# Second expert stage fed from attention's token order: its normalisation and logits beside and behind attention, half of its low weight halves kept in DRAM

## The chip, the cores and the metric

The kernel runs on one core of a Trainium2 chip. The metric is the device time of one execution in microseconds (us): before the change the median of three runs is 1264.93 us (1262.17 to 1265.98). The engines of the core run side by side, each through its own list of instructions, and wait for each other by semaphores: TensorE (PE) for matrix products and transposes, VectorE (DVE), ScalarE (ACT), GpSimd (POOL), and SyncE (SP), which here only starts transfers. POOL starts the indirect ones.

## The reference, cut to what matters

Six blocks, each on a layer norm of x (4 x 512 tokens of 256 numbers), each added to x. The change touches the attention (second) and the experts (first and third, with the same weights).

```python
x = x + 0.5 * ffn(layernorm(x), gate_w, gate_b, w1, b1, w2, b2)    # experts, stage 0
x = x + attn(layernorm(x), Wqkv, bqkv, Wout, bout)                 # causal attention, 16 heads
x = x + 0.5 * ffn(layernorm(x), gate_w, gate_b, w1, b1, w2, b2)    # experts, stage 1
x = x + 0.5 * hadamard_ffn(layernorm(x), W1, W2, W3)
x = x + feature_attn(layernorm(x), ...)
x = x + 0.5 * hadamard_ffn(layernorm(x), W1, W2, W3)

def ffn(x, gate_w, gate_b, w1, b1, w2, b2):
    logits = x @ gate_w.T + gate_b                 # 8 experts
    top_vals, top_idx = top_k(logits, 2)
    routing = softmax(top_vals)
    for e in range(8):
        h = x @ w1[e].T + b1[e]                    # 256 -> 512
        y = h[:, 0::2] * sigmoid(1.702 * h[:, 0::2]) * (h[:, 1::2] + 1.0)
        out += (y @ w2[e].T + b2[e]) * weight_of(routing, top_idx, e)
```

## The kernel before, in words

All matrix products that matter are exact to about fp32: each operand is split into a high half (rounded, made by ACT) and a low half (the rest, made by DVE), and three of the four products are summed.

x stays in the core's memory (SBUF) as 16 tiles of 128 tokens, four tiles to a "batch" (b = 0 to 3). In stage 0 and in attention tile t holds tokens t*128 to t*128+127 ("token order", `by_tiles`). Stage 1 and what follows want partition p to hold 16 neighbouring tokens (`by_sixteens`). So at its end attention writes x to DRAM (`x_turned`, L988), waits, reads it back in the other order (L992), waits again, and only then does the stage close. Every stage ends in a barrier of all engines in which its semaphores are cleared.

An expert stage (`experts_stage`, `which` = 0 or 1) runs like this. SP loads the small constants and eight records of weights (768 KB each, `record`, L410) and stores the normalised rows xn (L415). For each batch DVE makes the statistics (L91, L96), POOL the reciprocal root (L102, L105), DVE normalises (L114), PE transposes (L125), ACT and DVE split (L131, L136), PE computes the gate products (L484 to L489), ACT copies them out (L625), PE adds and transposes them to logits (L498), and DVE picks the best two (`choose`, L712 to L722). When all four batches are chosen, a routing chain on DVE and PE (L749 to L836) sorts 4096 token copies into 40 slots of 128 rows, one expert each. POOL then gathers the rows of xn by index (L456), two slots to a pair, and PE runs through 20 pairs (`turn`, `first`, `turn_y`, `second`), after which POOL scatters the results to DRAM (L462). Before the first pair PE waits for all eight low weight halves (`lo_split`, DVE L706: two in `choose`'s neighbourhood, two during the token sums, four after the indices), for the bias rows, and for the owners of the slots. At the end SP reads the results back (L431) and DVE adds them to x with the routing weights (L910).

Attention goes through 96 steps, three to each pair of heads, 24 (`WIDTH`) to each batch; `ALL` is 96. In step t, PE makes the scores (L1139), DVE their maxima (L1487); seven steps later (`LAG`) PE makes the transposed scores (L1154), ACT the exponentials (L1366), POOL masks them (L1041), and later still PE weighs the values (L1169). The steps also carry the projections of the next batch and the tail (sums, context, output projection, addition to x) of the last. Steps 96 to 107 are the drain, in which only the late parts of batch 3 run; behind the loop follow batch 3's sums (L1179), context (L1186), output projection (L1196) and addition (L1514). The order on each engine is the order in which the code is written, step by step; no scheduler moves anything.

Of the kernel before, what the change touches and what calls it, by code (L numbers as in the profile page):

```python
# [14 lines left out]
P = 128  # L15
# [29 lines left out]
def f32(ap):  # L45
    return ap.bitcast(F32)
# [22 lines left out]
class Norm:  # L69
# [28 lines left out]

    def rstd(self, pool, b):
# [39 lines left out]

def program(nc, ins, out):  # L140
# [4 lines left out]
    with ExitStack() as ctx:  # L145
# [23 lines left out]
        g.minus_low = sb("minus_low", [P, 1])  # L169
        g.xn_dram = nc.dram_tensor("xn_rows", (TOKENS, D), F32, kind="Internal").ap()  # L170
# [100 lines left out]
def experts_stage(nc, g, ins, which, x_dram):  # L271


    with ExitStack() as ctx:
# [5 lines left out]
        gate_w = sb("gate_w", [P, KC, E])  # L280
        gate_r = sb("gate_r", [P, KC, 2, E], F32R)
        both = sb("both", [2 * E, E])
        across = sb("across", [2 * E, 2, SEQ])
        b1_all = sb("b1_all", [P, E, 2 * IC])
        gate_b = sb("gate_b", [P, E])
        iota = sb("iota", [P, E])
        logits = sb("logits", [P, TILES, E])
        top = sb("top", [P, TILES, 8])
        top_at = sb("top_at", [P, TILES, 8], U32)
# [57 lines left out]
        rec_here = [sem(f"rec_here{e}") for e in range(E)]  # L347
        b1_here, b1_filled = sem("b1_here"), sem("b1_filled")
        pool_const, hi_split, lo_split, zeroed = sem("pool_const"), sem("hi_split"), sem("lo_split"), sem("zeroed")
        gate_split, logits_ready, logits_added = sem("gate_split"), sem("logits_ready"), sem("logits_added")  # L350
        gates_ps, gates_out, both_done = sem("gates_ps"), sem("gates_out"), sem("both_done")
        top_done, at_done = sem("top_done"), sem("at_done")
# [14 lines left out]
        norm = Norm(nc, sem, g, "norm", BATCH)  # L367
# [23 lines left out]
        def _(sp):  # L391
            if which == 0:
# [5 lines left out]
            sp.dma_start(gate_w[:, :, :], ins["gate_w"]).then_inc(small_here, 16)  # L398
            sp.dma_start(gate_b[:, :], ins["gate_b"].rearrange("(a e) -> a e", a=1).partition_broadcast(P)) \
                .then_inc(small_here, 16)  # L400
            sp.dma_start(iota[:, :], ins["iota"]).then_inc(small_here, 16)
            sp.wait_ge(zeroed, 1)
            for r in (0, LO_ROW):
                sp.dma_start(b2_src[r:r + E, :], ins["b2"]).then_inc(b2_here, 16)

            sp.dma_start(b1_all[:, :, :], ins["moe"].rearrange("e p n -> p e n")[:, :, REC_W1 + REC_W2:REC]) \
                .then_inc(b1_here, 16)

            def record(e):
                sp.dma_start(f32(w[1][:, e, :]), ins["moe"][e][:, 0:REC_W1 + REC_W2]).then_inc(rec_here[e], 16)  # L410
            for e in range(E // 2):
                record(e)
            for b in range(BATCH):
                sp.wait_ge(norm.xn_done, b + 1)
                sp.dma_start(by_tiles(g.xn_dram[:, :], b), g.xn[:, b, :, :]).then_inc(xn_stored, 16)  # L415
                record(E // 2 + b)
            sp.wait_ge(owner_done, 1)
            for j, (hi, _, source) in enumerate(jobs):
                if j:
                    sp.wait_ge(later_hi, j)  # L420
                    sp.wait_ge(later_lo, j)
                sp.dma_start(later[:, 0:hi.shape[1]], source).then_inc(later_here, 16)
            if which == 1:
                sp.dma_start(w3_raw[:, :, :], ins["w3"]).then_inc(w3_here, 16)
            for s in range(2):
                sp.wait_ge(scattered[s], 16 * PAIRS)
            for b in range(BATCH):
                if b >= 2:
                    sp.wait_ge(combined, 2 * (b - 1) + 1)
                for r in range(2):  # L430
                    sp.dma_start(back[:, b % 2, r, :, :], by_tiles(g.made_dram[r * TOKENS:(r + 1) * TOKENS, :], b)) \  # L431
# [1869 lines left out]
```

## Time and profile before

| | us |
|---|---|
| median of three runs | 1264.93 |
| the profiled execution, its own time | 1265.17 |
| its span, first to last instruction | 1263.4 |
| PE busy over the span | 1038.3 (82%) |
| DVE, ACT, POOL busy | 737.3, 461.0, 448.0 |

The stages follow each other without overlap. In the profiled execution stage 0 runs until about 227 us, attention until about 549 us, stage 1 until about 773 us, and the rest is the Hadamard and feature stages. A row of the timeline gives start, busy time, engine, line, operation, output and inputs, how many instructions were merged into it (x8), and in brackets how long the engine had been idle before it and which instruction ended that wait. A SPq row is SP starting a transfer, not the transfer. PEclk is the granted clock of PE, 1.0 being 2.4 GHz and 0.5 being 1.2 GHz.

### The profile page before, as it was taken

How to read it: one execution, taken by the hardware profiler on the slowest of the kernel's cores; microseconds unless marked ns; L12 is line 12 of the kernel's file. 1: busy time of each engine (PE TensorE's matmuls, PEld its weight loads, DVE VectorE, ACT ScalarE, POOL GpSimd, SP SyncE). 2: the span in 40 equal slices, each digit the busy share in tenths (PEclk: the TensorE clock that was granted, in tenths of full speed). 3: DMA queues.
4: the chain of work that ended last, by engine and by line, in shares of the span. 5: the costliest groups of instructions: out<-in, count | busy, mean ns of one | idle time of the engine just before them, and what ended most of it. 6: DMA issues, size and time to landing. Idle time of an engine off the chain costs nothing. (4 is left out here: it accounts for less than half of the span.)

```text
span 1263.4 us, 18069 instructions
## 1 busy us (share of the span) xinstructions
PE 1038.3 (82%) x6196; PEld 844.0 (67%) x6196; DVE 737.3 (58%) x1753; ACT 461.0 (36%) x804; POOL 448.0 (35%) x482
## 2 busy tenths in 40 slices
PE   4469992459999999624599993999989999789997
PEld 3358882346566666313488882888878888678886
DVE  5854443457777777157454436565646667655554
ACT  3314331127666766224143321322323333222231
POOL 2046652435353622120366630000127879500000
PEclk9579997667999999765699996999986999989999
DMA  9013224000000000082142233000010030000001
GB/s 333 3 59 110 88 80 160 22 1 1 2 1 18 1 18 5 30 244 91 46 173 86 89 113 105 1 1 1 1 67 1 1 67 1 1 1 17 18 6 29
DMA packets 38524, 66.03 MB, mean 52 GB/s; under 512 B 8195, under 2 KB 29732, under 8 KB 38054
## 3 DMA queue, kind: packets, MB, share of 16 engines
q1 hardware_dynamic: 30758, 43.90, 10.9%
q0 software_dynamic: 7680, 20.98, 5.1%
q8 instruction: 54, 0.88, 0.3%
q14 instruction: 32, 0.26, 0.1%
HBM read 43.89 MB, written 20.97 MB: 51 GB/s over the span
## 5 line engine op out<-in xcount | busy, mean ns | idle before, releaser
L1698 PE MATMUL ps<-xt,w 128*128 128x512 f32 x768 | 194.4, 404 | 5.6 <-PEq L66 3.2
L1698 PEld LDWEIGHTS ps<-xt,w 128*128 128x128 f32 x768 | 143.9, 193 | 36.5 <-DVE xt L136 6.2
L1487 DVE CUSTOM_DVE_ANT_0 ps<-ps,att_mask 128x128 f32<-128x128 f32 (+3 forms) x256 | 119.1, 516 | 39.7 <-PE ps L1139 39.5
L559 PE MATMUL ps<-moe_w,moe_narrow_xb 128*128 x480 | 126.8, 400 | 0.0
L456 POOL DMA_INDIRECT moe_xs<-xn_rows,moe_index x80 | 81.0, 1012 | 129.2 <-DVE moe_index L836 85.7
L1794 DVE TENSOR_TENSOR had_gated<-ps,had_sig 128x512 f32<-128x512 f32 x64 | 44.2, 691 | 120.1 <-ACT had_sig L1751 120.1
L102 POOL TENSOR_TENSOR var_eps<-bn,eps 128x4 f32<-128x4 f32 x24 | 5.2, 218 | 297.3 <-DVE bn L96 297.3
L462 POOL DMA_INDIRECT made_rows<-moe_units_made,moe_index x80 | 81.2, 1015 | 77.4 <-ACT moe_units_made L669 65.2
L1751 ACT ACTIVATE had_sig<-ps 128x512 f32<-128x512 f32 x64 | 38.4, 600 | 187.0 <-PE ps L1698 187.0
L559 PEld LDWEIGHTS ps<-moe_w,moe_narrow_xb 128*128 128x128 f32 x480 | 92.7, 194 | 19.2
L853 DVE TENSOR_TENSOR moe_narrow_xb<-ps,moe_narrow_xb 128x512 fp32r<-128x512 f32 x40 | 27.7, 692 | 128.9 <-ACT moe_narrow_xb L651 128.9
L1366 ACT ACTIVATE att_early_probs<-ps 128x384 f32<-128x384 f32 (+1 forms) x192 | 90.9, 527 | 29.0 <-PE ps L1154 27.7
L1710 PE MATMUL ps<-w,had_yhi 128*128 128x256 f32 x512 | 93.3, 280 | 1.8 <-DVE had_ylo L1806 1.8
L1041 POOL TENSOR_SCALAR_AFFINE_SELECT att_early_probs<-att_early_probs 128x256 f32<-128x256 f32 x128 | 53.3, 429 | 114.2 <-ACT att_early_probs L1366 113.9
L651 ACT ACTIVATE moe_narrow_xb<-ps 128x512 fp32r<-128x512 f32 x40 | 23.9, 598 | 177.9 <-PE ps L543 177.9
L1710 PEld LDWEIGHTS ps<-w,had_yhi 128*128 128x128 f32 x512 | 82.4, 188 | 8.0 <-DVE had_ylo L1806 2.6
L1139 PE MATMUL ps<-att_kt,att_q 48*128 48x128 f32 (+3 forms) x256 | 65.5, 413 | 9.4 <-DVE att_q_stack L1487 6.8
L2004 PE MATMUL ps<-fea_wv_prod,ident 128*128 128x256 f32 x256 | 68.3, 429 | 5.0 <-DVE fea_wv_prod L2194 5.0
L1710 PE MATMUL ps<-w,had_ylo 128*128 128x256 f32 x256 | 71.7, 280 | 0.0
L1924 POOL TENSOR_TENSOR fea_inv_norm<-fea_norm,neg_half 128x24 f32<-128x24 f32 x16 | 66.7, 4172 | 5.7 <-DVE fea_norm L2152 5.7
L585 PE MATMUL ps<-moe_w,moe_units_yb 128*128 x480 | 68.7, 283 | 0.0
L2004 PEld LDWEIGHTS ps<-fea_wv_prod,ident 128*128 128x128 f32 x256 | 54.2, 216 | 15.0 <-DVE fea_wv_prod L2194 6.2
(249 smaller groups left out, 2266.9 us busy)
## 6 DMA issues: line engine op xcount, KB each, us to landing
moe_w<-in_moe SPq DMA_DIRECT2D x16, 768.0 KB, 8.6
moe_w<-made_rows SPq DMA_DIRECT2D x16, 512.0 KB, 4.9
xn_rows<-moe_wide_xn SPq DMA_DIRECT2D x8, 512.0 KB, 9.5
x<-x_turned SPq DMA_DIRECT2D x8, 512.0 KB, 7.8
x<-in_x SPq DMA_DIRECT2D x4, 512.0 KB, 5.4
x_turned<-x SPq DMA_DIRECT2D x4, 512.0 KB, 2.9
moe_narrow_later<-in_w SPq DMA_DIRECT2D x4, 512.0 KB, 3.4
x_turned<-x SPq DMA_DIRECT2D x1, 2048.0 KB, 8.2
```

The costliest lines, as they stand in the source:

```text
L456: nc.gpsimd.indirect_dma_start(out=xs[:, j % 2, i, :], out_offset=None, in_=g.xn_dram[:, :], in_offset=at(0, 2 * j + i)).then_inc(gathered ...
L462: nc.gpsimd.indirect_dma_start(out=g.made_dram[:, :], out_offset=at(1, 2 * j + i), in_=made[:, j % 2, i, :], in_offset=None) \
L559: last = nc.tensor.matmul(h_bank(j, i), xb[a][:, j % 2, i, k, :], weight(c), start=False, stop=(k == KC - 1 and c == 1))
L585: last = nc.tensor.matmul(O_BANK[:, i * D:(i + 1) * D], yb[a][:, j % 2, i, c, :], weight(q), start=False, stop=(c == IC - 1 and q == 1), s ...
L1041: last = nc.gpsimd.affine_select(block, block, [[0, 2], [1, P]], ALU.is_ge, 0.0, base=0, channel_multiplier=-1)
L1139: last = nc.tensor.matmul(g.ps[:, a, col:col + n], q1[at, w % 2, i * P:n], kt[at, w % 4, 0:n], start=True, stop=True)
L1366: nc.scalar.activation(probs[:, w % 3, a, at:at + n], g.ps[:, 2 + a, 0:n], ACT.Exp, scale=HD ** -0.5).then_inc(exp_done, 1)
L1487: last = nc.vector.tensor_tensor_reduce(g.ps[:, a, col:col + n], g.ps[:, a, col:col + n], mask[:, SEQ - n:SEQ], -1.0, 3.0e38, ALU.add, ALU ...
L1698: last = nc.tensor.matmul(g.ps[:, bank(n, half), :], w[a][:, k, c * P:(c + 1) * P], xt[low][:, b % 2, k, :], start=(k == 0 and q == 0), st ...
L1710: last = nc.tensor.matmul(o, a[:, n % 4, at], g.w2[w][:, c, :], start=(c == 0 and q == 0 and i % 2 == 0), stop=(c == HC - 1 and q == 2), s ...
L1924: nc.gpsimd.tensor_tensor(inv_norm[:, t % 4, :], norm2[:, t % 4, :], g.neg_half[:, 0:QKH], ALU.pow) \
L2004: last = nc.tensor.matmul(g.ps[:, 5 + t % 2, 0:D], g.ident[:, :], wv_prod[:, t % 2, k, :, :].rearrange("p h d -> p (h d)"), start=(k == 0) ...
```

## The change

- **Token order.** Routing of stage 1 is made in attention's token order. Attention no longer reads x back at its end; SP reads it in the other order in the middle of stage 1's expert loop, after the second of the later weights. The results are read back `by_sixteens`. The routing weights, made in token order, are turned by a small way round: PE transposes them (32 x 128), ACT copies them out, SP stores them to DRAM and loads them back in the other order (`route_rows`, `route_back`).
- **Normalisation for stage 1 moves into attention**, as a second `Norm` named `after` and a class `Choice` with the four steps from gate products to the best two. For batches 0 and 1 DVE makes it in pieces, one after the maxima of each step of the last batch (u = 1 to 8 and 9 to 16): four of one tile's statistics, one for the variances, one empty, two of two tiles' normalisation. Batch 2 follows in steps 97 and 100. Transposes, splits, gate products, logits and choice of batches 0 to 2 stand in the drain (`AFTER`: they begin at steps 97, 99 and 102, the gate products two steps later, the logits three). Batch 3 has all of it behind attention's last addition. The normalised rows take the place of attention's own and of `rot`.
- **Low halves.** Stage 0, once its eight low halves are made, writes those of experts 4 to 7 to DRAM (`low_weights`). Stage 1 reads them back instead of making them, and makes only four on DVE.
- **Order within stage 1.** SP starts with the records. ACT makes the routing weights and then the eight high halves and the biases. PE turns the biases after the token sums. DVE makes the bias rows after the owners.

The diff, cut:

```diff
@@ Norm @@
+    def stats_of_tile(self, b, i, x_block):
+        self.nc.vector.bn_stats(self.g.bn6[:, self.slot(b), i, :], x_block(i)).then_inc(self.stats_done, 1)
+    def variance(self, dve, b, stats_done):       # bn_aggr x4
+    def normalise_tiles(self, b, tiles, x_block): # tensor_scalar for each tile
+class Choice:    # gates, out_of_gates, logits_of, choose: the code of experts_stage, moved
@@ experts_stage, SP @@
+            def stored_low(e):
+                sp.dma_start(f32(w[1][:, e, :]), g.low_dram[e - E // 2]).then_inc(low_here[e], 16)
+            else:
+                record(0)
+                record(1)
+                biases()
+                for e in range(2, E):
+                    record(e)
+                for e in range(E - LOADED, E):
+                    stored_low(e)
+                sp.wait_ge(rows_out, 1)
+                sp.dma_start(g.route_dram, route_rows[:, :]).then_inc(rows_stored, 16)
+                sp.wait_ge(rows_stored, 16)
+                sp.dma_start(route_back[:, :, :], ...).then_inc(route_here, 16)
             sp.wait_ge(owner_done, 1)
+            if which == 0:
+                sp.wait_ge(lo_split, E)
+                for e in range(E // 2, E):
+                    sp.dma_start(g.low_dram[e - E // 2], f32(w[1][:, e, :])).then_inc(low_stored, 16)
...
+                if which == 1 and j == 1:
+                    for b in range(BATCH):
+                        sp.dma_start(g.x[:, mine, :], by_sixteens(g.turned_dram[0])[:, mine, :]).then_inc(x_here[b], 16)
@@ experts_stage, PE @@
-            pe.wait_ge(lo_split, E)
+            if which == 1:
+                turn_biases()
+                pe.wait_ge(route_done, 2)
+                nc.tensor.transpose(g.ps[0:2 * TILES, 7, 0:P], route[...], g.ident[:, :]).then_inc(route_turned, 1)
+            pe.wait_ge(hi_split, E)
+            pe.wait_ge(lo_split, E - LOADED)
+            if which == 1:
+                for e in range(E - LOADED, E):
+                    pe.wait_ge(low_here[e], 16)
@@ attention_stage @@
+        AFTER = ((5, ALL + 1), (0, ALL + 3), (5, ALL + 6), (2, None))
-            for b in range(BATCH):
-                at = slice(b * BATCH_P, (b + 1) * BATCH_P)
-                sp.dma_start(g.x[at, :, :], by_sixteens(g.turned_dram[0])[at]).then_inc(x_turned, 16)
-            sp.wait_ge(x_turned, 16 * BATCH)
+            for b in range(BATCH):
+                sp.wait_ge(xn_stored[b], 16)
@@ PE, in the loop @@
+                for m in at_step(t, 3):
+                    choice.logits_of(pe, m, bank_of(m) + 1)
+                for m in at_step(t, 2):
+                    choice.gates(pe, m, bank_of(m))
+                for m in at_step(t, 0):
+                    turn_after(m)
+            pe.wait_ge(choice.gates_out, 2)
+            pe.wait_ge(choice.logits_added, 2)
@@ DVE, in the loop @@
+                for m in range(2):
+                    if 0 <= u - 1 - 8 * m < 8 and b == BATCH - 1:
+                        after_piece(m, u - 1 - 8 * m)
@@ DVE, behind the loop @@
+            after_whole(BATCH - 1)
+            after.low(dve, BATCH - 1, bank_of(BATCH - 1), xt[0][:, :, :], xt[1][:, :, :])
+            choice.choose(dve, BATCH - 1, bank_of(BATCH - 1) + 1)
```

On PE, the end of the drain and what is behind it stood like this before (`att_summed` are batch 3's weighted values, `wout` the output projection):

```order
L1154 MATMUL ps<-att_q,att_kt 128x128
L1169 MATMUL ps<-att_early_probs,att_v 17x128 x4
L1169 MATMUL ps<-att_early_probs,att_v 17x256 x4
L1169 MATMUL ps<-att_early_probs,att_v 17x384 x4
L1169 MATMUL ps<-att_early_probs,att_v 17x512 x4
L1179 MATMUL ps<-ident,att_summed 128x128 x16
L1186 MATMUL ps<-ident,att_context 128x128 x8
L1196 MATMUL ps<-wout,att_ct 128x256 x24
```

The same place now (`att_turns_after_xn` are rows normalised for stage 1, `gate_r` the split gate weights, `both` the small matrix that adds the two halves of the gate products):

```order
L197 MATMUL ps<-both,att_qk 128x8 x4
L142 MATMUL ps<-ident,att_turns_after_xn 128x128 x8
L1318 MATMUL ps<-att_early_probs,att_v 17x128 x4
L1318 MATMUL ps<-att_early_probs,att_v 17x256 x4
L178 MATMUL ps<-att_xt,gate_r 16x512
L180 MATMUL ps<-att_xt,gate_r 8x512 x2
L182 MATMUL ps<-att_xt,gate_r 16x512
L1318 MATMUL ps<-att_early_probs,att_v 17x384 x4
L1318 MATMUL ps<-att_early_probs,att_v 17x512 x4
L197 MATMUL ps<-both,att_qk 128x8 x4
L1328 MATMUL ps<-ident,att_summed 128x128 x16
L1335 MATMUL ps<-ident,att_context 128x128 x8
```

Batch 2's transposes, gate products and logits now stand between and around the last weighings; those of batches 0 and 1 stand the same way further up.

On DVE, between the slot rows and the first pair of the expert loop of stage 1, before:

```order
L816 TENSOR_TENSOR moe_wide_slot_row<-column,moe_pos 128x2048 x2
L706 TENSOR_TENSOR moe_w<-moe_w 128x1536 x2
L823 TENSOR_SCALAR moe_narrow_index_f<-ps 128x40
...
L846 TENSOR_SCALAR moe_owner_row<-moe_owner,row_e 128x40
L706 TENSOR_TENSOR moe_w<-moe_w 128x1536 x4
```

And now:

```order
L931 TENSOR_TENSOR moe_wide_slot_row<-column,moe_pos 128x2048 x2
L826 TENSOR_TENSOR moe_w<-moe_w 128x1536 x3
L938 TENSOR_SCALAR moe_narrow_index_f<-ps 128x40
...
L961 TENSOR_SCALAR moe_owner_row<-moe_owner,row_e 128x40
L859 SCALAR_TENSOR_TENSOR moe_b_row<-moe_units_b_hi,minus_low,ps 128x512
L861 SCALAR_TENSOR_TENSOR moe_b_row<-moe_units_b_hi,minus_low,moe_units_b_src 128x256
L826 TENSOR_TENSOR moe_w<-moe_w 128x1536
```

Three low halves stand ahead of the indices, and one, with the bias rows ahead of it, behind the owners, where there were four.

On SP, stage 1 from its start to the first of the later weights, now:

```order
L491 DMA moe_w<-in_moe 128x1536 x2
L499 DMA moe_units_b_src<-in_b 8x256 x2
L500 DMA moe_b_all<-in_moe 128x8x4
L491 DMA moe_w<-in_moe 128x1536 x6
L494 DMA moe_w<-low_weights 128x1536 x4
L523 DMA route_rows<-moe_route_rows 32x128
L525 DMA moe_route_back<-route_rows 128x2x16
L536 DMA moe_narrow_later<-in_had 128x256
```

Before, the small constants stood first, then four records, and each of the other four stood behind the store of one batch of normalised rows.

## Rows read from the trace of the kernel before

**Rows 1.** Timeline, seam from attention to stage 1: start, us, engine, what, [idle before].
```profile
532.36 0.69 DVE L1514 TENSOR_TENSOR x<-x,ps 128x512 f32<-128x512 f32 x1 [1.14 <-PE ps L1196]
...
549.38 1.40 DVE L91 BATCH_NORM_STATS2 bn<-x 128x6 f32<-128x256 f32 x4 [16.34 <-PEq L66]
```

**Rows 2.** Timeline of stage 1, POOL and PE, at the start of the expert loop.
```profile
604.91 1.09 POOL L456 DMA_INDIRECT moe_xs<-xn_rows,moe_index  x1 [41.97 <-DVE moe_index L836]
606.30 1.79 POOL L456 DMA_INDIRECT moe_xs<-xn_rows,moe_index  x1 [0.30 <-issue]
612.33 1.11 PE L543 MATMUL ps<-ident,moe_xs 128*128 128x128 f32 x4 [9.49 <-DVE moe_w L706]
```

**Rows 3.** Timeline of stage 1, DVE, from batch 3's logits to the low halves.
```profile
583.39 0.18 DVE L712 TENSOR_TENSOR moe_logits<-ps,moe_gate_b 128x32 f32<-128x32 f32 x1
584.57 0.17 DVE L749 TENSOR_TENSOR moe_margin<-moe_top 128x16 f32<-128x16 f32 x1
602.88 0.20 DVE L823 TENSOR_SCALAR moe_narrow_index_f<-ps 128x40 f32<-128x40 f32 x1 [1.57 <-PE ps L528]
605.52 6.76 DVE L706 TENSOR_TENSOR moe_w<-moe_w 128x1536 fp32r<-128x1536 f32 x4
```

**Rows 4.** Stretches: start:end, length; busy (count) of five engines, PEclk, DMA share, GB/s.
```profile
453.00:503.00 50.00, 48.55 (x395) 30.31 (x393) 39.35 (x147) 33.59 (x69) 12.63 (x32) 1.00 0.04 12
503.00:521.50 18.50, 14.07 (x91) 5.54 (x89) 0.69 (x1) 8.30 (x17) 3.92 (x10) 0.72 0.09 29
613.00:749.00 136.00, 126.61 (x756) 109.51 (x755) 58.84 (x87) 49.75 (x86) 76.58 (x76) 0.97 0.29 98
```

**Rows 5.** Stage 1, groups by shape, 549 to 586 us: xcount | busy us, mean ns.
```profile
L91 DVE BATCH_NORM_STATS2 bn<-x 128x6 f32<-128x256 f32 x16 | 5.6, 410 | 16.3 <-PEq L66 16.3
L114 DVE TENSOR_SCALAR moe_wide_xn<-x,bn,rstd 128x256 f32<-128x256 f32 x16 | 5.4, 402 | 0.0
L96 DVE BATCH_NORM_AGGREGATE bn<-bn 128x2 f32<-128x6 f32 x16 | 1.6, 159 | 0.6 <-issue 0.2
```

**Rows 6.** Timeline of stage 1: transposes, low split, gate products, copy and logits of single batches.
```profile
555.01 1.97 PE L125 MATMUL ps<-ident,moe_wide_xn 128*128 128x128 f32 x8 [22.75 <-DVE moe_gate_r L740]
558.07 1.22 DVE L136 TENSOR_TENSOR moe_narrow_xt<-ps,moe_narrow_xt 128x1024 fp32r<-128x1024 f32 x1
559.69 0.78 PE L484 MATMUL ps<-moe_narrow_xt,moe_gate_r 128*16 128x512 f32 x1
561.78 0.59 ACT L625 ACTIVATE moe_across<-ps 16x512 f32<-16x512 f32 x1 [0.68 <-PE ps L489]
562.41 1.10 PE L125 MATMUL ps<-ident,moe_wide_xn 128*128 128x128 f32 x8 [0.67 <-DVE moe_wide_xn L114]
564.58 1.05 PE L498 MATMUL ps<-moe_both,moe_across 16*128 16x8 f32 x8
579.81 1.87 PE L498 MATMUL ps<-moe_both,moe_across 16*128 16x8 f32 x8
```

**Rows 7.** Timeline, PE: weighings L1169, 16 in the loop and 32 after it.
```profile
496.59 1.70 PE L1169 MATMUL ps<-att_early_probs,att_v 128*17 128x384 f32 x16
516.39 4.47 PE L1169 MATMUL ps<-att_early_probs,att_v 128*17 128x128 f32 x32 [1.41 <-POOL att_early_probs L1041]
```

**Rows 8.** Timeline of DVE over the barrier between stage 1 and the next stage.
```profile
773.41 1.40 DVE L91 BATCH_NORM_STATS2 bn<-x 128x6 f32<-128x256 f32 x4 [1.23 <-PEq L66]
```

**Rows 9.** Stretches as in Rows 4, while weights and rows move.
```profile
555.00:575.00 20.00, 13.39 (x60) 8.78 (x60) 13.90 (x58) 9.86 (x10) 3.03 (x6) 0.74 1.03 390
561.00:563.00 2.00, 1.33 (x7) 0.59 (x6) 2.00 (x7) 1.32 (x3) 1.70 (x4) 0.76 0.88 259
573.00:575.00 2.00, 0.00 (x0) 0.00 (x0) 1.93 (x14) 0.52 (x1) 0.00 (x0) 1.00 1.10 431
```

**Rows 10.** Gathers L456, all 80 of them.
```profile
DMA to landing us min/median/max: 2.6/2.8/5.5
```

**Rows 11.** Timeline of DVE at the end of stage 1: the additions wait for the results.
```profile
756.48 6.67 DVE L910 SCALAR_TENSOR_TENSOR x<-moe_w,moe_route,x 128x256 f32<-128x256 f32 x16 [6.99 <-DMA moe_w<-made_rows]
```

More of the change, by code:

```diff
@@ L440, in _ @@
             pool.wait_ge(zeroed, 1)
-            for b in range(BATCH):
-                norm.rstd(pool, b)
+            if which == 0:
+                for b in range(BATCH):
+                    norm.rstd(pool, b)
             pool.wait_ge(b1_here, 16)
@@ L493, in logits_of @@
-            def logits_of(b):
-                pe.wait_ge(gates_out, b + 1)
-                if b >= 2:
-                    pe.wait_ge(logits_added, b - 1)
-                for i in range(BT):
-                    last = nc.tensor.matmul(g.ps[:, b % 2, i * E:(i + 1) * E], across[:, b % 2, i * P:(i + 1) * P],
-                                            both[:, :], start=True, stop=True)
-                last.then_inc(logits_ready, 1)
-            norm.turn(pe, 0, 4)
-            norm.turn(pe, 1, 6)
@@ L818, in _ @@
                     .then_inc(spread, 1)
-            for e in range(2, 4):
+            for e in range(2 - 2 * which, 4 - which):
                 low_weights(e)
@@ L847, in _ @@
                 .then_inc(owner_done, 1)
-            for e in range(4, E):
+            if which == 1:
+                bias_rows()
+            for e in range(4 - which, E - LOADED):
                 low_weights(e)
@@ L1379, in high_context, with high_after @@
                 nc.scalar.activation(ct[0][:, k, :], g.ps[:, bank, :], ACT.Copy).then_inc(chi_done, 1)
+            def high_after(m):
+                if m == 0:
+                    act.wait_ge(v_ps, 4 * BATCH)
+                else:
+                    act.wait_ge(choice.gates_ps, m)
+                after.high(act, m, bank_of(m), xt[0][:, :, :])
             act.wait_ge(consts, CONSTS)
@@ L1583, in _ @@
                     maxima(t)
+                for m in range(2):
+                    if 0 <= u - 1 - 8 * m < 8 and b == BATCH - 1:
+                        after_piece(m, u - 1 - 8 * m)
+                for m in at_step(t, 3):
+                    choice.choose(dve, m, bank_of(m) + 1)
+                for m in at_step(t, 0):
+                    after.low(dve, m, bank_of(m), xt[0][:, :, :], xt[1][:, :, :])
+                if t == ALL + 1:
+                    for piece in range(BT + 1):
+                        after_piece(2, piece)
+                elif t == ALL + 4:
+                    for piece in range(BT + 1, BT + 4):
+                        after_piece(2, piece)
             for i in range(BT):
```

449 lines of the change are left out of this document (303 added, 146 removed).

## The prediction

> **What bounds the kernel now.** I read the busy tenths by slice first, then the busy time by stretches, then the timeline of all engines over the seam between attention and stage 1. Attention's steps and both expert loops are bound by PE: in the steps of the last batch PE is busy 48.55 of 50 us, and in stage 1's loop 126.61 of 136 [rows 4]. At the seam nothing of the sort holds. DVE's last addition of attention ends at 533.05 us. Then x goes to DRAM and comes back (L988, L992), and DVE starts stage 1 at 549.38, having stood still for 16.3 us [rows 1]. The normalisation and the choice of four batches last until DVE's L749 at 584.57; the routing chain leads to the index at 602.88 and the first gather at 604.91; and the first transposes of the expert loop start at 612.33, held by the last four low halves (605.52 + 6.76 = 612.28) [rows 2, 3]. So from 533.05 to 612.33, 79.3 us, the kernel hangs on a chain of waits and PE mostly stands still. The change is about this chain, and its worth is the move of the time 612.33.
>
> **The chain after the change**, link by link, on the clock of the trace of before.
>
> First, *attention until 533.05*. In the last batch's steps DVE gets the pieces of two batches: statistics, variances and normalisation cost 5.6 + 1.6 + 5.4 = 12.6 us for four batches [rows 5], so 6.3 us for two. DVE is busy 39.35 us of those 50 [rows 4] and has 10.65 us free, but PE, with 1.45 us free, waits for DVE's maxima of the step before, so a piece in a step where DVE is late shows. I take 1 us; the ends are 0 (all in the gaps) and 6.3 (all exposed). POOL's part hides, since POOL is busy 12.63 of the 50.
>
> *The drain* (503 to 521.5) gets PE's, ACT's and DVE's work of three batches. Transposes, gate products and logits of one batch run without a gap from 562.41 to 564.58 + 1.05 = 565.63, which is 3.22 us at the upper clock; at the lower one they are 1.97 + (561.78 - 559.69 = 2.09) + 1.87 = 5.93 us [rows 6]. Three batches are 9.7 or 17.8 us. What can hide them: PE stands idle for 18.5 - 14.07 = 4.4 us of the drain, and its granted clock falls there to 0.72 [rows 4]. The 32 weighings of the last group take 4.47 us, while 16 of them at the upper clock took 1.70 [rows 7], so about 1.3 us, and as much again for the first group, come back if denser work keeps the clock up. The low end is 9.7 - 4.4 - 2.6 = 2.7 us, the high end 17.8. I take 5: near the low end, as PE gets work where it stood idle, yet above it, since ACT and PE hand the exponentials to and fro and new instructions stand between them in both orders; the last gate products and logits stand among the last weighings, with nothing to hide in. DVE, at 0.69 us busy, has room for all of its part. With the 1 us of the steps, the last addition ends at 533.05 + 6 = 539.1.
>
> *Batch 3* then has its whole chain alone. In stage 1 the same way took from 549.38 (statistics) over the transposes at 555.01 to the end of the low split at 558.07 + 1.22 = 559.29, 9.9 us; gate products to the end of the copy 561.78 + 0.59 - 559.69 = 2.7; logits 1.87; choice 584.57 - 583.39 = 1.2 [rows 1, 3, 6]. With three handovers of 0.05 it is 15.8 us, at the lower clock: PE will have been without work for some 6 us when the transposes come, as before those of 555.01, which ran at it. Were all of PE's part at the upper clock, 5.93 - 3.22 = 2.7 us would go. Attention ends at 539.1 + 15.8 = 554.9. Storing the last rows is started about 5 us after the addition and lies beside the other 10. The barrier costs 1.23 us [rows 8], so DVE starts stage 1 at 556.1 instead of 549.38. What was gained by leaving out the turn of x (16.3 us) is thus about paid away by batch 3's chain and the drain: minus 6.7.
>
> *Routing* starts at once. From L749 to the first gather took 604.91 - 584.57 = 20.3 us [rows 2, 3]. A third low half ahead of the index costs 0.1: DVE waited 1.57 us there, and a half takes 6.76 / 4 = 1.69 [rows 3]. The bias rows that stood ahead of the scan lay beside PE's ranks, so they give nothing. The first gather goes out 20.5 us after the stage's start, its partner 1.4 later, and it lands after 2.8 [rows 2, 10]: the rows of the first pair are there after 24.7 us. The biases are made on ACT behind the eighth high half (about 21 us, as records arrive), DVE's bias rows and last low half then end at about 25. These two ends fall together.
>
> *The weights* are the third. Stage 1 now moves twelve blocks of 128 x 1536 x 4 B = 0.786 MB, 9.44 MB in all, where it moved eight and four stores. While such transfers kept the DMA engines full, from 555 to 575, they moved 390 GB/s; two stretches of it moved 259 and 431 [rows 9]. At 390 GB/s it is 24.2 us. Ahead of it I put 2 us from start to first bytes and 1 for the tiny bias pieces, behind it 1 for landing: 28.2 us. At 431 it would be 25.9, at 259 it would be 40.4. The four low halves come last in SP's queue and PE waits for all of them, so my value is that they end the wait: the first transposes at 556.1 + 28.2 = 584.3. That is 28.0 us before 612.33.
>
> The trace gives 390 GB/s [rows 9]. The Trainium skill (DMA: Bandwidth & Descriptors, Bandwidth) holds that HBM limits such reads to about 358 GB/s for one core; this trace is above that, so the row decides, and by the page's figure the load would take 26.4 us and the sum be 2.2 us higher. By another section of that page (Issuing engines are not separate DMA queues), POOL's gathers run on the same 16 engines as SP's transfers and interleave with them; no row of before shows the two together here, and by it the first gathers would land later without being last.
>
> **The rest.** Stage 0 writes 3.1 MB: some 8 us of transfers at the start of its loop. Stage 1's loop gets 2 MB of x and the small way round of the routing weights. In stage 1's loop the DMA share is 0.29 with PE busy 93% of the time [rows 4], so there is room: 0, up to 3 if gathers come late. Behind the loop DVE waited 6.99 us for the results [rows 11]; they now come in pieces of 4 KB instead of 1 KB. I take 0.5 us less, between 1.5 less and 1 more. The ceiling is that DVE and ACT still have to turn the other weights.
>
> **The sum**, against the profiled execution's own 1265.17 (0.24 above the median of 1264.93): 1265.17 - 28.0 - 0.5 = 1236.7, so 1237 us.
>
> **Rivals.**
> *A: the weights are not last.* For it: full stretches at 431 GB/s bring the load to 25.9 us, and gathers and DVE end near 25. Against: the mean over 20 us is 390. The loop would start at about 25.5 instead of 28.2: 1237 - 2.7 = 1234. With PE at the upper clock in batch 3's chain too it would be 1231.5.
> *B: attention pays more.* The drain is paid at the lower clock (13.7 after what little hides) and the steps at half their pieces (3). For it: the clock of 0.72 in the drain, and ACT, which is one list for exponentials and the new copies. Against: PE's idle 4.4 us. That is 16.7 instead of 6: 1237 + 10.7 = 1248.
> *C: slower than before, by the weights.* In before four of the eight low halves cost DVE 6.8 us at the end; now they are 3.1 MB more to read, behind everything. The point from which it decides is a first transposes later than 612.8, 56.7 us into the stage: 9.44 MB in 52.7 us, 179 GB/s. At 150 GB/s, 63 us, it would be 1265.17 + 10 - 0.5 = 1275. For it: rates fell to 259 once, and the low halves are read from a buffer that no row shows being read. Against: that stretch was 2 us long, and the reads have 6 KB a partition like the records.
> *D: the seam does not shorten*, because batches 0 to 2 wait in the drain for each other and everything lands behind the loop: from transposes to choice a batch takes 15.8 - 5.6 (549.38 to 555.01 [rows 1, 6]) = 10.2 us, three of them 30.6 in place of my 5: 1262.6, within what can be told. Against: the steps between them give each hop one or two steps of time.
>
> **How the numbers follow.** The forecast, weights last and 4 to 9 us paid in attention, has 0.55, from 1233 to 1241; A 0.17; B 0.22; C 0.03; D 0.03. The range has to leave out no more than 2 in 10: it goes from 1229 to 1249, taking in A whole and most of B. A measurement of this kernel can tell about 0.3%, 3.8 us, from no change. Slower by more than that is C, 0.03; within it D and the neighbourhood, 0.02; the rest, 0.95, is faster.
>
> **What would show it.** In the profile after: the last addition of x at about 539, with PE's clock in the drain over 0.8; the first rows of stage 1's DVE at about 556, an idle time of about 1.2 before them; the first gather 20 to 21 us later, and PE's first transposes of gathered rows 28 us later, put down to a transfer of `moe_w`, not to DVE; the distance from there to the end of the kernel as before, less about half a us. It is wrong if the steps of the last batch grow by more than 3 us, if the drain grows by more than 9, if the wait ahead of the expert loop ends with the gather or with a low half made by DVE (A), or if the loop itself, 613 to 745 before, is no longer of the same length.

## The result and the profile after

The changed kernel takes 1253.33 us (median of 20 runs, 1246.21 to 1262.62), the one before 1265.43 (20 runs); the ratio is 0.9898, interval 0.9881 to 0.9915. It is faster, by 1.0% instead of the 2.2% forecast: 1253.3 lies above 1237 and above the range's end of 1249. The profiled execution took 1256.92 us with a span of 1254.7.

First the timeline of the seam (start, us, engine, what, idle before), which answers to [rows 1, 6, 8]:

```profile
555.70 0.69 DVE L1700 TENSOR_TENSOR x<-x,ps 128x512 f32<-128x512 f32 x1 [1.87 <-PE ps L1345]
561.12 1.94 PE L142 MATMUL ps<-ident,att_turns_after_xn 128*128 128x128 f32 x8 [5.53 <-issue]
565.50 0.61 PE L178 MATMUL ps<-att_xt,gate_r 128*16 128x512 f32 x1 [2.43 <-DVE att_xt L153]
568.06 1.87 PE L197 MATMUL ps<-both,att_qk 16*128 16x8 f32 x8 [0.68 <-ACT att_qk L189]
572.41 0.19 DVE L865 TENSOR_TENSOR moe_margin<-top 128x16 f32<-128x16 f32 x1 [1.17 <-PEq L66]
...
592.32 1.09 POOL L579 DMA_INDIRECT moe_xs<-xn_rows,moe_index  x1 [10.78 <-DVE moe_index L951]
600.31 1.08 PE L653 MATMUL ps<-ident,moe_xs 128*128 128x128 f32 x4 [8.39 <-DMA moe_w<-low_weights]
```

The last addition of attention ends at 556.39, where 539.1 was forecast. From there the chain runs as forecast: 16.0 us to stage 1's first work on DVE at 572.41 (17.0 forecast), 19.9 to the first gather (20.5), 27.9 to the first transposes of gathered rows (28.2), and these wait for the transfer of the low halves, as forecast. Before, the way from the last addition to these transposes was 79.3 us; now it is 43.9. The seam works. What was lost was lost ahead of it, in attention.

The stretches of attention (start:end, length; busy and count of PE, weight loads, DVE, ACT, POOL; PE's granted clock, DMA share, GB/s) answer to [rows 4]. They run from one batch's last addition to the next: batch 2's steps, batch 3's steps, the drain; then stage 1's load and the stretch of the loop in which x is read:

```profile
395.00:459.70 64.70, 62.77 (x468) 42.32 (x468) 46.36 (x158) 42.56 (x88) 28.86 (x49) 0.95 0.03 9
459.70:518.00 58.30, 55.56 (x396) 33.95 (x396) 44.80 (x172) 33.95 (x70) 15.06 (x36) 0.85 0.08 28
518.00:555.70 37.70, 32.06 (x192) 20.22 (x192) 15.26 (x67) 13.50 (x25) 5.06 (x12) 0.73 0.09 28
...
576.40:598.40 22.00, 8.17 (x37) 7.69 (x37) 19.75 (x29) 12.81 (x11) 6.84 (x6) 0.50 1.01 398
...
623.00:640.00 17.00, 14.15 (x77) 12.17 (x76) 6.97 (x11) 6.25 (x10) 8.90 (x9) 0.90 0.68 248
```

The same three stretches of attention in the kernel before:

```profile
391.60:453.40 61.80, 59.81 (x468) 39.85 (x468) 46.32 (x159) 42.45 (x88) 28.89 (x49) 1.00 0.03 10
453.40:503.40 50.00, 48.55 (x394) 30.31 (x394) 39.38 (x148) 33.59 (x69) 12.63 (x32) 1.00 0.04 12
503.40:532.40 29.00, 21.32 (x136) 12.28 (x134) 5.12 (x13) 9.41 (x19) 3.92 (x10) 0.76 0.06 19
```

PE does the same matmuls in the steps of batch 3, yet is busy for 55.6 us instead of 48.6: its granted clock is 0.85 instead of 1.00 (of the two levels, 2.4 GHz all the time before, and 1.2 GHz for part of it now). DVE has 5.4 us more to do, where the prediction counted 6.3. PE's own standing still grew by only 1.3 us, and the view of waits of PE in this stretch (what waited for what: us in total, times, longest) names it. First after, then before:

```profile
PE ps L1258 <- DVE att_kt L1663: 1.3, 3, 0.7
PE ps L1288 <- DVE att_q_stack L1673: 0.7, 3, 0.3
```

```profile
PE ps L1139 <- DVE att_q_stack L1487: 0.7, 3, 0.3
```

New are three waits for DVE's copy of K into `kt` (L1663). PE waits for it because the copy reads the bank of the accumulator memory (PSUM) into which PE's next transposes (L1258) go. The copy opens every third step, so eight of them stand among the 24 steps. In six of them one of the new pieces stands right ahead of the copy, and in three of these six the copy comes late. The longest wait, with the normalisation of two tiles ahead of the copy:

```profile
497.98 0.82 DVE L112 TENSOR_SCALAR att_turns_after_xn<-x,bn,rstd 128x256 f32<-128x256 f32 x2
498.72 0.68 DVE L1663 CAST att_kt<-ps 128x512 fp32r<-128x512 f32 x1
499.54 0.63 PE L1258 MATMUL ps<-ident,att_q_stack 128*128 128x128 f32 x4 [0.69 <-DVE att_kt L1663]
```

The loop itself (first transposes to SP's last request for results) has grown from 137.1 to 140.2 us, and in it PE waits once for a gather, while x is read:

```profile
PE ps L653 <- DMA moe_xs<-xn_rows,moe_index: 2.4, 1, 2.4
```

At the loop's end DVE waits 5.97 us for results instead of 6.99 [rows 11].

### The profile page after: what moved, and what is told of

It reads as the page before. It is cut to its first block and busy times, and to the rows that moved or that the text cites. A ratio compares the mean times of both kernels' runs of the same rounds, so it can differ in the third digit from the quotient of the medians.

```text
span 1254.7 us, 18084 instructions
## 1 busy us (share of the span) xinstructions
PE 1052.2 (84%) x6197; PEld 855.9 (68%) x6197; DVE 728.8 (58%) x1745; ACT 462.3 (37%) x805; POOL 450.5 (36%) x482
## 5 line engine op out<-in xcount | busy, mean ns | idle before, releaser
L1927 PE MATMUL ps<-xt,w 128*128 128x512 f32 x768 | 191.6, 400 | 5.6 <-PEq L66 3.2
L1288 PE MATMUL ps<-att_kt,att_q 48*128 48x256 f32 (+3 forms) x256 | 66.8, 428 | 9.8 <-DVE att_q_stack L1673 7.2
```

Source lines behind the costliest of these rows:

```text
L1288: last = nc.tensor.matmul(g.ps[:, a, col:col + n], q1[at, w % 2, i * P:n], kt[at, w % 4, 0:n], start=True, stop=True)
L1927: last = nc.tensor.matmul(g.ps[:, bank(n, half), :], w[a][:, k, c * P:(c + 1) * P], xt[low][:, b % 2, k, :], start=(k == 0 and q == 0), st ...
```

## The experiments

Theory 1: DVE's pieces and the added work in the drain cost attention what is missing, the pieces mostly by way of PE's granted clock; and x's 2 MB cost the loop 3 us. Its rival: these executions had a poorer clock by chance, and the pieces lie in DVE's gaps. All times are medians; ratios are against the kernel before on the same chip. "Steps" are those of batch 3, "drain" is from batch 2's last addition to batch 3's.

**e1_no_pieces**
```
 def after_piece(m, piece):
+    if m < 2:
+        if piece == BT: nc.vector.bn_aggr(...)      # one, to release POOL
...
+if t in (ALL, ALL + 1):                             # start of the drain
+    after.normalise_tiles(t - ALL, range(BT), ...)
```


> Leaves out, of batches 0 and 1, the statistics and variances, and takes their normalisation (from old statistics) out of the steps of the last batch and puts it at the start of the drain, where DVE is idle. All else is as in the changed kernel. Theory 1 (the pieces on DVE show in the steps): the 24 steps of the last batch, from batch 1's last addition to batch 2's, took 50.0 us before and 57.9 after; here they come back by most of the 6.3 us that the pieces cost DVE, to about 52, and the whole takes about 1247 us. Theory 2 (the steps were slow because the granted clock was lower in this execution, by chance or because PE waited a little more, and the pieces lie in DVE's gaps): the steps stay above 56 us wherever the granted clock in them is below 0.9, and the whole stays at about 1253.

1248.38 us, ratio 0.9878 (0.9841 to 0.9915). The steps:

```profile
451.10:502.50 51.40, 49.99 (x394) 31.11 (x394) 39.55 (x149) 33.53 (x69) 15.06 (x36) 0.97 0.03 11
```

51.5 us with the clock at 0.97, and the waits for L1663 are gone, so theory 1 holds for the steps. The drain, into which the normalisation of two batches was moved, took 38.3 us in this execution.

**e2_no_drain**
```
-for m in at_step(t, 3): choice.logits_of(pe, m, bank_of(m) + 1)
-for m in at_step(t, 2): choice.gates(pe, m, bank_of(m))
-for m in at_step(t, 0): turn_after(m)
...                                                  # ACT's and DVE's parts too
```


> Leaves out, in the drain, the transposes, the split, the gate products, the logits and the choice of batches 0 to 2 (batch 3's are made as before and take batch 0's place); the pieces on DVE stay. Theory 1 (work that goes into the drain is paid for nearly in full, 8.7 us where 5 were forecast): from batch 2's last addition to batch 3's it is 29 us again instead of 37.7, and the whole takes about 1244.5 us. Theory 2 (the drain is longer because PE's granted clock fell in it to 0.77 and its chain of hand-overs between PE, ACT and DVE has the same length without the added work): it stays at 33 us or more and the whole takes 1249 or more.

1241.23 us, ratio 0.9789 (0.9754 to 0.9824), 12.1 below the changed kernel. The drain:

```profile
518.90:545.20 26.30, 18.83 (x132) 11.38 (x132) 8.34 (x24) 9.12 (x19) 5.08 (x12) 0.87 0.12 41
```

26.4 us: less than the 29.0 of before, at a better clock. So the added work costs 8.6 us against the 35.0 that the drain takes in five of the six executions whose attention is that of the changed kernel (below). Theory 1 holds: 26.4 us is even below the 29 that it expected. The steps here took 61.0 us at a clock of 0.80, with the three waits: these have nothing to do with the drain.

**e8_again** (the changed kernel once more)

> The changed kernel once more, word for word. If the steps of the last batch are slow by the change itself, they take 57 to 59 us again with PE's granted clock at 0.85 to 0.88; if that was the chance of one execution, they come out nearer to the 50.0 us of before. The way from the loop's first transposes to SP's last request for results is 140 us again if it is the change's, 137 if it was chance. The whole: 1253.

1252.42 us, ratio 0.99 (0.9855 to 0.9944).

```profile
389.30:454.00 64.70, 62.74 (x466) 42.31 (x467) 46.38 (x158) 42.54 (x88) 28.83 (x49) 0.95 0.03 9
454.00:515.00 61.00, 58.15 (x396) 35.05 (x396) 45.12 (x171) 34.00 (x70) 15.07 (x36) 0.80 0.08 27
515.00:550.00 35.00, 29.30 (x192) 19.88 (x192) 15.30 (x67) 13.55 (x25) 5.04 (x12) 0.81 0.09 31
```

The long steps are the change's, not one execution's. The drain's 37.7 us was partly chance: here it is 35.0, 6.0 more than before. The loop takes 140.6.

**e10_before_again** (the kernel before once more)

> The kernel before once more, word for word. Its profiled execution had attention's last 24 steps in 50.0 us and the loop of the second expert stage in 137.1. If the change made both longer, they come out at 50 to 51 and at 136.5 to 137.5 again; if chance of an execution did, at least one of them moves towards the changed kernel's 57 to 61 and 140 to 141. The whole: 1265.

1267.98 us, ratio 1.0011 (0.9979 to 1.0043).

```profile
455.40:505.40 50.00, 48.19 (x388) 29.84 (x386) 39.38 (x148) 33.80 (x70) 12.63 (x32) 1.00 0.04 12
505.40:534.50 29.10, 21.09 (x132) 12.39 (x132) 5.16 (x13) 9.08 (x19) 3.92 (x10) 0.77 0.06 19
613.81:752.25 138.44, 129.49 (x761) 113.06 (x762) 59.27 (x87) 49.75 (x86) 76.66 (x76) 0.95 0.29 96
```

50.0 and 29.0 us again, to 0.05. The loop is 138.4, so part of its 3 us may be chance of one execution: this point came out between the two outcomes.

**e5_fine**
```
-for m in range(2):
-    if 0 <= u - 1 - 8 * m < 8 and b == BATCH - 1: after_piece(m, u - 1 - 8 * m)
+for m, piece in {2 * WIDTH + 3: ((0, 0),), 2 * WIDTH + 4: ((0, 1),), ...
+                 3 * WIDTH + 3: ((0, 5),), 3 * WIDTH + 5: ((0, 6),), ...
+                 ALL: ((1, 5), (1, 6), (1, 7), (1, 8))}.get(t, ()):
+    fine_piece(m, piece)                            # one tile each
```


> Nothing is left out; DVE's pieces of batches 0 and 1 are placed anew. Batch 0's statistics and variances go into the steps of batch 2, its normalisation goes tile by tile into the steps of batch 3, never into a step right ahead of one that opens with the copy of K (L1663), batch 1's statistics likewise, and batch 1's normalisation goes to the start of the drain. In the changed kernel PE waited three times for that copy (1.3 us) and its granted clock was 0.85 in these steps. Theory 1 (the pieces cost through those waits: PE stands still for a moment and its granted clock falls behind each, so that PE's busy time grows from 48.6 to 55.6 us): without the waits the steps from batch 1's last addition to batch 2's come back to 50 to 52 us, as where the pieces were left out, and the whole takes about 1247 us. Theory 2 (any 6 us more on DVE, wherever they lie, slow PE by lateness of the maxima): the steps stay above 55 us and the whole at 1251 or more.

1246.12 us, ratio 0.9848 (0.9807 to 0.9889).

```profile
391.80:456.30 64.50, 62.46 (x468) 42.13 (x467) 48.33 (x167) 42.68 (x88) 30.33 (x51) 0.95 0.03 10
456.30:506.70 50.40, 48.95 (x394) 30.22 (x394) 41.71 (x160) 33.60 (x69) 14.03 (x34) 1.00 0.07 22
```

The cut leaves out the matching move of POOL's reciprocal roots. DVE still does 2.3 us of new work in the steps (and 2 us in those of batch 2), but the steps take 50.4 us at the full clock, and the waits for L1663 are gone: PE's waits in this stretch are those of before.

```profile
PE ps L1288 <- DVE att_q_stack L1673: 0.7, 3, 0.3
```

Over all profiled executions: in six without the waits for L1663 the steps took 50.0 to 52.0 us (50.0, 50.0, 50.4, 51.5, 51.8, 52.0); in eight with them 57.5 to 61.0, at clocks from 0.80 to 0.88. Theory 1 holds. One rival is not excluded: this run also leaves less than half of DVE's 5.4 us in these steps (the rest went to batch 2's steps and the drain), so placement and amount were changed together, and no run has all of it in these steps clear of the copies.

The traces tell in which order waits and clock came. In the profiled run of the changed kernel the waits for L1663 ended at 472.23, 486.24 and 499.54, and PE's clock fell in three stretches:

```profile
463.90:467.30 3.40, 3.40 (x29) 2.13 (x28) 1.52 (x6) 1.20 (x3) 0.45 (x2) 0.50 0.01 2
474.10:480.90 6.80, 6.80 (x39) 3.84 (x40) 5.12 (x19) 3.48 (x8) 2.47 (x5) 0.50 0.01 2
501.40:508.20 6.80, 6.80 (x38) 4.85 (x42) 4.31 (x17) 4.54 (x10) 1.58 (x4) 0.50 0.00 0
```

The second and the third stretch begin 1.9 us behind a wait. So it is in all eight executions with the waits: each stretch of 6.8 us at 0.50 in these steps begins 1.5 to 3.0 us behind one of them, and 18 of the 24 waits have one. The first stretch above stands ahead of the first wait. Four of the eight have such a short one there, and e1_no_pieces, e11_fine_tail and e12_fine_three_tail have one each without any wait for L1663, with steps of 51.5 to 52.0 us. So 1.5 to 2 us of the profiled run's 8.3 need not come from these waits (an estimate from those lengths).

What theory 1 does not explain are batch 2's steps. PE has the same waits there in either kernel (the longest 0.7 to 0.8 us), and except in the three runs with finer pieces their code is unchanged. Yet they took 61.8 us in both executions of the kernel before and 63.4 to 64.9 in all twelve others, with the mean clock at 0.95 to 0.97 instead of 1.00. The 2.9 us that they cost in the profiled run stay open.

**e7_tail**
```
 turn_context(BATCH - 1, 1, 6)
+turn_after(2)
 project_half(BATCH - 1, 0, 0)
 project_half(BATCH - 1, 1, 1)
+choice.gates(pe, 2, bank_of(2))
+choice.logits_of(pe, 2, bank_of(2) + 1)
```


> Batch 2's transposes, gate products, logits and choice are moved out of the drain's last weighings to behind the context of batch 3, where its output projection and the statistics of batch 3 are under way; nothing is left out. Theory 1 (PE's work that was added to the drain is paid nearly in full at the low clock, and batch 3's chain behind it has gaps of 5.5 and 2.4 us in which PE waits): from batch 2's last addition to the choice of batch 3, 52.6 us in the changed kernel, 2 to 3 us are saved and the whole takes about 1250.5. Theory 2 (the chain of hand-overs is the bound, not PE): the same length within 1 us, 1253.

1244.29 us, ratio 0.9841 (0.98 to 0.9882). The timeline of PE at the end of attention shows batch 2's transposes (first line) between context and projection, and its logits ahead of batch 3's transposes:

```profile
543.28 1.04 PE L142 MATMUL ps<-ident,att_turns_after_xn 128*128 128x128 f32 x8
545.02 3.14 PE L1345 MATMUL ps<-wout,att_ct 128*128 128x256 f32 x24 [0.70 <-DVE att_ct L1695]
548.00 0.40 PE L178 MATMUL ps<-att_xt,gate_r 128*16 128x512 f32 x1
549.76 1.05 PE L197 MATMUL ps<-both,att_qk 16*128 16x8 f32 x8 [0.68 <-ACT att_qk L189]
553.69 1.94 PE L142 MATMUL ps<-ident,att_turns_after_xn 128*128 128x128 f32 x8 [2.88 <-issue]
```

What stood in the way of the drain now fills a gap of batch 3's chain: PE stands still for 2.88 us ahead of that batch's transposes instead of 5.53, and the work there runs at the upper clock (1.04 us for eight transposes, 1.94 at the lower one). From batch 2's last addition to batch 3's choice it is 45.7 us, 4.0 less than in e8_again: theory 1, by more than its 2 to 3 us. The median fell by 8.1; the rest I can't place, since in the profile it lies in later, unchanged stages (506.6 us after SP's request, 512.9 in e8_again, 506.4 in e10_before_again), which vary that much by themselves.

**e3_all_low**
```
-LOADED = E // 2 if which == 1 else 0
+LOADED = 0                                          # and no store in stage 0
```


> No low half goes to DRAM: all eight are made by DVE in stage 1 as before the change, four of them after the bias rows; stage 0 stores none and stage 1 reads none back. Theory 1 (weights last, as the prediction had it): the load is then 6.3 MB instead of 9.4 and no longer last; DVE ends last: the low half that ended at 594.92 + 1.75 = 596.7 is followed by 6.8 us of four more, so the first transposes of gathered rows come 31 us after the stage's start instead of 27.9, 3.1 us more, put down to DVE. Against it stand the 1.7 us that stage 0 grew by, if its stores caused them: the whole takes 1253.3 + 3.1 - 1.7 = 1254.7 us. Theory 2 (the stores cost stage 0 nothing and what it grew by is chance): 1256.4 us, stage 0 as long as in the changed kernel.

1254.56 us, ratio 0.9909 (0.9878 to 0.9939), the same within the error.

```profile
597.37 1.08 PE L651 MATMUL ps<-ident,moe_xs 128*128 128x128 f32 x4 [11.54 <-DVE moe_w L824]
```

That is 31.05 us after the stage's start at 566.32, held by DVE: theory 1's 31. Keeping low halves in DRAM is thus worth 3 us. Its store costs nothing that can be seen: from stage 0's first transposes of gathered rows to attention's start it is 157.6 us here and 156.7 to 158.2 in the eleven executions that store four halves or three. The 1.7 us that attention started late were chance; that part of theory 1 fell.

**e6_three**
```
-LOADED = E // 2 if which == 1 else 0
+LOADED = 3 if which == 1 else 0                     # and three stores in stage 0
```


> Three instead of four of the low halves go to DRAM and back; DVE makes the fifth in stage 1, behind the bias rows. Theory 1 (the prediction's: the load is last by far, and DVE would end at 26.0 us after the stage's start, 24.3 and 1.75): the load is 0.79 MB shorter, 2.0 us at 390 GB/s, so the first transposes come 26.0 us after the stage's start instead of 27.9, and the whole takes about 1251.5. Theory 2 (the load's rate is set by something that another low half on DVE or the gathers disturb, or DVE ends later than the sum): they come at 27 or later, and put down to DVE.

1252.01 us, ratio 0.9899 (0.9858 to 0.9939).

```profile
591.07 1.09 PE L653 MATMUL ps<-ident,moe_xs 128*128 128x128 f32 x4 [6.77 <-DVE moe_w L826]
```

26.3 us after the stage's start (564.80), against the forecast 26.0: theory 1 in the length, though DVE is now last. The median shows none of it: the loop of this execution took 142.0.

**e4_x_spread**
```
-if which == 1 and j == 1: (four reads of x, one behind the other)
+for b in range(BATCH):
+    sp.wait_ge(x_turned, 11 + 2 * b)
+    (the read of batch b)
```


> The 2 MB of x that stage 1's loop reads back at its second pair are asked for one batch at a time, behind pairs 11, 13, 15 and 17. Theory 1 (the block of 2 MB holds up the gathers of three pairs, whose rows PE waited 5.8 us for between 625 and 640): the way from the first transposes of the loop to SP's last request for results goes from 140.2 us to the 137.1 of the kernel before, and the whole takes about 1250.5 us. Theory 2 (the waits are only moved, since DVE and ACT's turned weights and PE set the loop's pace on average): it stays at 139 to 141 us and the whole at 1253.

1250.95 us, ratio 0.989 (0.9861 to 0.9919). The loop took 139.8 us, theory 2: the wait for the gather shrank from 2.4 to 0.7 us, and others grew (for L985 from 0.5 to 2.2).

**e9_no_x**
```
-sp.dma_start(g.x[:, mine, :], ...)                  # 512 KB a batch
+sp.dma_start(g.x[:, mine, 0:128], ...)              # mine: one tile; 64 KB
```


> Leaves out nearly all of the read of x in the second expert stage's loop: of each batch 64 KB instead of 512 KB come back. Spread over the loop, the 2 MB had cost it the same as in one block (139.8 us from the first transposes to SP's last request for results, 140.2 to 140.6 in the changed kernel, 137.1 before). Theory 1 (it is the 2 MB themselves, wherever they lie, that delay gathers, and results by about 3 us): the way is 137 to 138 us. Theory 2 (the loop is longer by something else, such as the order in which the turned weights' requests stand behind the gathers or the chance of the granted clock): it stays at 139.5 or more.

1247.79 us, ratio 0.9863 (0.9822 to 0.9904).

```profile
590.77:726.84 136.07, 127.31 (x761) 110.21 (x762) 59.15 (x86) 49.76 (x86) 76.78 (x76) 0.97 0.31 101
```

The loop takes 136.1 us, theory 1, and 1 us under its range; the eleven executions that read x back took 139.5 to 142.0, the two of before 137.1 and 138.4. So it is the 2 MB themselves, wherever they lie. Their price is known only roughly, from one execution without them: 3.4 to 5.9 us against these eleven, and 3.8 against e4_x_spread, whose loop had nearly the same clock (0.98 against 0.97).

**e11_fine_tail** (the edits of e5_fine and e7_tail together)

> Two edits together, nothing left out: DVE's pieces of batches 0 and 1 placed clear of the copies of K, and batch 2's part moved behind the context of batch 3. Alone they gave medians of 1246.1 and 1244.3 us against the 1252.4 of the changed kernel. Theory 1 (they act in different stretches, the one on the steps' granted clock, the other on the drain, and add up): 1252.4 - 6.3 - 8.1 = 1238 us. Theory 2 (both win back the same granted clock, or part of the second's gain was chance in the later stages, whose 506.6 us were 6 less than in the changed kernel's second profile): about 1242.

1238.97 us, ratio 0.9777 (0.9736 to 0.9818): the two edits add up, which is theory 1, with steps of 52.0 us and a drain of 30.2 us.

**e12_fine_three_tail** (that and the edit of e6_three)

> As the kernel with DVE's pieces clear of the copies of K and batch 2's part behind the context of batch 3, and in addition three instead of four low halves by way of DRAM. Theory 1 (the first transposes come 1.7 us earlier after attention's end, as they did with this edit alone, and the rest keeps its length): 1.5 us less than the kernel without this edit. Theory 2 (the loop that starts earlier finds its gathers later, since with this edit alone the loop took 142.0 us instead of 140.6): no difference.

1236.49 us, ratio 0.9762 (0.9719 to 0.9804).

```profile
459.70:511.50 51.80, 50.05 (x388) 30.76 (x386) 41.84 (x160) 33.79 (x70) 14.03 (x34) 0.97 0.06 22
511.50:541.00 29.50, 26.08 (x182) 16.93 (x183) 15.34 (x57) 12.53 (x24) 5.12 (x12) 0.83 0.16 54
```
```profile
583.80 1.08 PE L653 MATMUL ps<-ident,moe_xs 128*128 128x128 f32 x4 [6.55 <-DVE moe_w L826]
```

Steps and drain are as in e11_fine_tail. From stage 1's start (557.75) to these transposes it is 26.05 us. Against e11_fine_tail the two intervals overlap, so the 2.5 us between them are not shown by the times alone, and neither theory is decided by them; the 26 us instead of 28 are, by this trace and e6_three's. This version beats both kernels: 2.4% under the one before, 1.3% under the changed one. That it lands at the forecast's 1237 says nothing for the forecast, which was made for the changed kernel's order of work.

## Why the prediction missed

| link, us (+ longer or later than before) | forecast | profiled run | e8_again |
|---|---|---|---|
| start of attention | 0 | +1.7 | -1.9 |
| from there to batch 0's last addition | 0 | +1.7 | -0.4 |
| batch 2's steps | 0 | +2.9 | +2.9 |
| batch 3's steps | +1 | +8.3 | +11.0 |
| drain | +5 | +8.7 | +6.0 |
| last addition to stage 1's start, length | 17.0 | 16.0 | 16.0 |
| stage 1's start to first transposes, length | 28.2 | 27.9 | 28.2 |
| loop | 0 | +3.1 | +3.5 |
| end of stage 1 | -0.5 | -1.2 | -1.0 |
| later stages | 0 | +1.4 | -0.1 |

*The step that failed* is the first: "so a piece in a step where DVE is late shows. I take 1 us; the ends are 0 (all in the gaps) and 6.3 (all exposed)". The delay itself was sized rightly: PE waited 1.3 us more. But the bound of 6.3 held only for delays at an unchanged clock. The eight executions with the three new waits show 7.5 to 11.0 us, above that end, since PE's granted clock fell, mostly right behind these waits, and its 48.6 us of work became 54.1 to 58.2. And I did not look at which instruction stands behind a piece in DVE's queue: not only the maxima, but every third step the copy of K, which PE needs at once. The profile before showed both: PE 97% busy at a clock of 1.00, so with much to lose, and a clock of 0.72 in the drain, where it stands still. I had used the clock's rise as a gain in the drain and not its fall as a price in the steps. Two of the signs that I had named for being wrong came true: the steps grew by more than 3 us, and the loop did not keep its length.

*The drain*: 5 forecast, 6.0 in most executions, 8.7 in the profiled one; mis-sized by little. Its gain of clock by denser work came only in part: 0.81 in e8_again and 0.73 in the profiled run, against 0.76 before. The 1.3 us that I gave to the last weighings are 1.1 by my own rows (4.47 - 2 x 1.70) [rows 7]. e2_no_drain puts the added work at 8.6 us.

*x's way back*, "0, up to 3": the loop grew by 3.1 and 3.5 us, just above that end, and e9_no_x puts the cause at the 2 MB. The DMA share of 0.29 [rows 4] said that there was room on average; while x is read the share is 0.68, and the two gathers asked for then, at 625.1 and 626.4, took 7.0 and 6.6 us to land.

*Unchanged steps of batch 2*: 2.9 us in no term, and unexplained.

*Right*: batch 3's chain (14.9 us to its choice, 15.8 forecast), the barrier, routing, and the load, which was last, with DMA blamed. It moved 398 GB/s, gathers included, where I had taken 390. The Trainium skill's figure of about 358 GB/s for one core (DMA: Bandwidth & Descriptors, Bandwidth), which I had set aside for the row, is again below what this trace shows. The first three gathers of stage 1, asked for at 592.3 to 595.0 beside the end of the load, took these times to land, where the first three of before took 3.2 to 3.6 us:

```profile
DMA to landing us min/median/max: 5.3/5.9/6.0
```

Over all 80 gathers of after it reads as follows, the slowest being one of stage 0 beside the store of the low halves; before, the slowest took 5.5 [rows 10]:

```profile
DMA to landing us min/median/max: 2.6/2.8/7.9
```

That agrees with the rule of that page of the Trainium skill (DMA: Bandwidth & Descriptors, Issuing engines are not separate DMA queues) that they interleave with SP's transfers, and they were not last, as forecast. The store of the low halves cost nothing that can be seen (e3_all_low against the others).

*The rivals.* A is refuted for this kernel (DMA was last in each of the nine executions that load four low halves), but e6_three shows how near it was: one low half less, and DVE is last at 26.3. B named the right place, and its 16.7 us for steps and drain together are near the 17.0 of the profiled run. But that is luck, for its two terms miss in opposite ways: 3 us for the steps where 8.3 came, 13.7 for the drain where 8.7 came. Its cause (length on DVE and a cold drain) was not the steps' true one. C and D did not come. Put the measured terms into the forecast's sum (last addition +17.3 later than forecast, chain and load -1.3, loop +3.1, end -0.7, later stages +1.4) and 1236.7 becomes 1256.5; 1256.92 was measured. This shows only that no link is left out, as the terms are of the same execution.

## What to carry to other kernels

Where PE is busy 97% of the time at the full clock, price work put on the engine that feeds it not by its own length but by the waits that it causes, and bound each wait by what PE would lose if its clock fell behind it: here 1.3 us of waits came with 7.5 to 11 us. Look at what stands directly behind each new piece in its engine's queue, and put pieces one tile at a time, clear of the instruction that PE needs next. With that placement, and 2.3 of the 5.4 us of work left in the steps, they grew by 0.4 to 2 us; which of the two did it was not separated. Work for PE that must go near the end belongs where PE already waits (between context and last rows), not where the drain is one chain.

## What was unexpected of the hardware

The granted clock is repeatable in its pattern: the steps of batch 3 came out at 57.49, 57.50, 57.51 and 57.51 us in four kernels whose attention is that of the changed kernel (e3_all_low, e4_x_spread, e6_three, e9_no_x), at 58.3 and 61.0 in that kernel itself, and the drain at 34.97 to 35.01 in five executions. So these lengths gather at a few values and are not spread about a mean. And the same wait of 0.7 us in batch 2's steps was followed by a fall of the clock in the changed kernel (0.66 in a stretch of 5 us) and by none in the kernel before (1.00), twice each. What the engine had done earlier may matter, but no run here tells.
